# Copying the masked blocks ahead of the exponentials on ScalarE, in the fourth head of three groups

## The reference

```python
# 1: gated linear attention, 8 heads of 128
q, k = l2norm(x @ Wq), l2norm(x @ Wk)
v, alpha = x @ Wv, sigmoid(x @ Wg)
S = a_t[..., None] * S + k_t[..., None] * v_t[:, :, None, :]
o_t = einsum('bhkv,bhk->bhv', S, q_t)          # then o @ Wo
# 2: cross attention with the context
probs = softmax(x @ W.T @ ctx.T); out = probs @ ctx
# 3: two of eight small experts per sequence, chosen by a gate on the mean row
out = sum over the two of weight * (gelu(x @ down + b) @ up + b_up)
```

## Time and profile before

| | us |
|---|---|
| median of the runs | 489.06 |
| the profiled execution's own time | 488.91 |
| its span, first to last instruction | 486.8 |
| TensorE (PE) busy | 462.1 (95%) |
| VectorE (DVE) busy | 374.4 (77%) |
| ScalarE (ACT) busy | 337.6 (69%) |
| GpSimd (POOL) busy | 109.6 (23%) |
| mean granted TensorE clock | 0.988 of 2.4 GHz |

### The profile page before, as it was taken

One profiled execution on the slowest core, in us unless ns is written; L12 is line 12 of the kernel. 1 busy time (PEld: TensorE's weight loads), 2 busy tenths in 40 slices (PEclk: granted clock), 3 DMA queues, 4 the chain that ended last, 5 costly groups with the idle time before them and its releaser, 6 DMA issues. The chain is left out here.

```text
span 486.8 us, 24127 instructions
## 1 busy us (share of the span) xinstructions
PE 462.1 (95%) x10322; PEld 385.0 (79%) x10322; DVE 374.4 (77%) x1059; ACT 337.6 (69%) x800; POOL 109.6 (23%) x102
## 2 busy tenths in 40 slices
PE   1799999999999999999999999999999999999886
PEld 1588788887888788888888888887878888877674
DVE  4778896767779788896779788887579678887574
ACT  3858877766777776778757776678857776766613
POOL 1022232212222222233122221233212221232121
PEclk9989999999999999999999999999999999999979
DMA  8900000001001010013011010013010010002023
GB/s 314 349 11 5 3 5 3 5 3 44 6 3 46 3 47 4 3 49 90 3 46 47 2 48 3 3 27 109 4 46 3 4 42 7 5 25 67 0 52 123
DMA packets 15321, 20.17 MB, mean 41 GB/s; under 512 B 1264, under 2 KB 13040, under 8 KB 15216
## 3 DMA queue, kind: packets, MB, share of 16 engines
q1 hardware_dynamic: 13936, 14.43, 9.2%
q0 software_dynamic: 1280, 4.20, 3.2%
HBM read 16.53 MB, written 2.10 MB: 38 GB/s over the span
## 5 line engine op out<-in xcount | busy, mean ns | idle before, releaser
L507 ACT COPY states<-states 128x512 f32<-128x512 f32 x128 | 80.9, 632 | 54.8 <-DVE states L741 41.0
L419 POOL TENSOR_TENSOR rnorm<-norm_sq,neg_half 128x4 f32<-128x4 f32 x32 | 44.6, 1394 | 265.6 <-DVE norm_sq L804 265.6
L741 DVE TENSOR_TENSOR states<-states,spans 128x512 f32<-128x512 f32 x96 | 66.4, 692 | 8.9 <-ACT states L507 1.0
L1254 PEld LDWEIGHTS lo_bank<-states 128*32 128x32 f32 x5120 | 51.4, 110 | 23.1 <-issue 19.4
L1254 PE MATMUL lo_bank<-states 128*32 128x16 f32 (+1 forms) x5120 | 58.4, 188 | 0.0
L1243 PE MATMUL ring<-wv_sb,xnT 128*128 128x256 f32 x384 | 55.9, 295 | 1.2 <-DVE wv_sb L1010 1.0
L1230 PE MATMUL ring<-xnT,wk_sb 128*128 128x512 f32 x192 | 53.7, 416 | 2.3 <-DVE xnT L873 1.5
L1230 PE MATMUL ring<-xnT,wq_sb 128*128 128x512 f32 x192 | 53.4, 413 | 0.0
L1230 PE MATMUL ring<-xnT,wg_sb 128*128 128x512 f32 x192 | 51.3, 402 | 0.4 <-DVE wg_sb L1010 0.4
L1243 PEld LDWEIGHTS ring<-wv_sb,xnT 128*128 128x128 f32 x384 | 49.2, 193 | 1.9 <-DVE wv_sb L1010 1.1
L792 DVE COPY_PREDICATED blocks<-owned,lo_bank 128x64 f32<-128x64 uint32 (+1 forms) x160 | 41.0, 256 | 12.1 <-PE lo_bank L1254 7.6
(11 more groups left out here) (201 smaller groups left out, 834.0 us busy)
## 6 DMA issues: line engine op xcount, KB each, us to landing
x_buf<-x_dram SPq DMA_DIRECT2D x4, 512.0 KB, 4.0
ctxT_sb<-ctxT_dram SPq DMA_DIRECT2D x8, 256.0 KB, 4.1
ctx_sb<-ctx_dram SPq DMA_DIRECT2D x4, 512.0 KB, 4.3
out_dram<-x_mid SPq DMA_DIRECT2D x6, 256.0 KB, 2.5
states<-wk_dram SPq DMA_DIRECT2D x1, 1024.0 KB, 5.7
states<-wg_dram SPq DMA_DIRECT2D x1, 1024.0 KB, 7.9
states<-wq_dram SPq DMA_DIRECT2D x1, 1024.0 KB, 9.9
v_sb<-wv_dram SPq DMA_DIRECT2D x1, 1024.0 KB, 12.0
```

The lines of the kernel that those rows point to most:

```text
L419: nc.gpsimd.tensor_tensor(rnorm[:, m % 4, GB:2 * GB], norm_sq[:, GB:2 * GB], neg_half[:, GB:2 * GB], ALU.pow).then_inc(rk_set, 1)
L507: nc.scalar.copy(halves(l, 2 ** (l - 1), False), halves(l - 1, 2 ** (l - 1), False)).then_inc(carry_set, 1)
L741: nc.vector.tensor_tensor(halves(l, w, True), halves(l - 1, w, True), by, ALU.mult).then_inc(decayed, 1)
L1254: last = mm(lo_bank[BLOCK * r:BLOCK * r + BLOCK, to:to + columns], view(states, left + start, [[1, BLOCK]]), view(states, right + start, q ...
```

## The change

In the heads with h = 3 from the second group on (n = 11, 19, 27), ScalarE issues `expand_blocks(n - 1)` directly behind `carry(n, 5)`, ahead of the exponentials and of alpha. In all other heads it stays behind alpha. The instructions, their waits and the semaphores that they signal are the same; no other engine's program changes.

```diff
                 carry(n, 5)
+                blocks_first = n % H == 3 and n > H
+                if blocks_first:
+                    expand_blocks(n - 1)
                 tail_part(n, "early")
                 if n + 1 < U:
                     alpha_out(n + 1)
-                if n >= 1:
+                if n >= 1 and not blocks_first:
                     expand_blocks(n - 1)
                 tail_part(n, "mid")
```

## The result

The changed kernel takes 486.65 us (median of 22 runs, 484.24 to 492.26). The kernel before, run beside it, takes 489.42 us (median of 22, 486.97 to 493.51). The ratio is 0.9936 with a 95% interval of 0.9918 to 0.9953. Put on the 489.06 us of the first three runs that is 485.9 us (485.0 to 486.8), where 487.2 was forecast with a range of 486.5 to 488.4. The direction was right, the gain was put too small: 1.85 us, against 2.3 to 4.0 by the interval. The ratio is formed from the runs that are not over 1.5% above the fastest, and it is not the ratio of the two medians: those are 2.8 us apart, 0.9943.

What follows compares the result with a forecast made beforehand. TensorE was taken to bound the kernel, waiting at L1324 for ScalarE's square in heads 11, 19 and 27; removing 0.75 + 0.68 + 0.42 = 1.85 us from 489.06 gave 487.2 us, range 486.5 to 488.4.

Steps and rivals of the forecast that it cites:

- What bounds the kernel: TensorE, busy 95% of the span; its wait at L1324 for ScalarE's square, three times, 1.8 us in all.
- The copies in their new place: On ScalarE ahead of the exponentials, 1.21 us of copies hide in the wait for VectorE's maxima; cost 0, at most 0.3.
- The rule on the drain behind a table load: The skill's 1.38 us drain after ScalarE's table load would make the exponentials late; as a rival 488.3 us, chance 0.03.
- The place that they leave: Behind alpha on ScalarE, the square ends 1.21 us earlier, so L1324's whole wait goes: 1.85 us, bounds 1.15 to 1.85.
- What is late next: VectorE's scaled output and the split of `xT` for TensorE's next products: both stay in time, margins 0.13 and 0.31 us.
- the first rival: VectorE comes no earlier and stops L1392 for 0.35 us in heads 11 and 19; gain 1.15, 487.9 us, chance 0.07.
- The margin of 0.13: Slack left for VectorE's scaled output before TensorE's `cross` 1 needs it: 0.40 + 0.48 - 0.75 us.
- the sum's last one: Whole kernel: median 489.06 less the three waits' 1.85 gives 487.2 us, 0.38% faster; forecast's chance 0.80.
- The fifth rival: Slow clock from 468 to 477 us falls on other work: 1.6 us less (485.6) or more (488.8), chance 0.04.

Runs made afterwards that it cites:

- g_overfill: Changed kernel plus four filler copies directly behind the masked copies, ahead of the exponentials, in heads 11, 19 and 27; ratio 0.9959 to the kernel before, median 487.98 us.
- b_hold: Changed kernel plus four filler copies behind alpha, in the place the masked copies left, heads 11, 19, 27; ratio 0.9998 to the kernel before, median 489.47 us.
- c_square_first: Kernel before with the masked copies of heads 11, 19 and 27 moved later, behind q's copy and square; ratio 0.9997 to the kernel before, median 491.97 us.
- e_max_only: Kernel before, masked copies unmoved, with VectorE's row maxima ahead of the two decays in heads 11, 19, 27; ratio 0.9910 to the kernel before, median 486.12 us.
- a_same: The kernel before, unedited, run against itself to measure noise; ratio 0.9979, medians 489.60 and 489.67 us.
- h_max_only: Second run of row maxima first on VectorE, masked copies where they were in the kernel before; ratio 0.9926 to the kernel before, median 486.26 us.

## Why the prediction was wrong, point by point

- **What bounds the kernel**: right. TensorE's wait at L1324 was the only one that the change touched, and it vanished in all three heads.
- **The copies in their new place cost nothing**: right. The idle time left before the exponentials is 1.18, 1.26 and 0.41 us, for 1.16, 1.18 and 0.33 forecast. g_overfill shows that the cover is real and where it ends.
- **The rule on the drain behind a table load**: the trace decides against it. In the changed kernel's head 11 the load ends at 163.57 and the exponentials wait for the maxima; in g_overfill nothing but the load is ahead of them, and they start 0.02 us behind its end. A drain of 1.38 us as in the Trainium skill ("ScalarE: Activation LUTs", "What ACT_TABLE_LOAD costs") would have shown there.
- **The place that they leave**: the mechanism was right (b_hold, c_square_first). The term was 0.75 + 0.68 + 0.42 = 1.85 and measured 0.83 + 0.73 + 0.45 = 2.01, and 2.16 and 1.80 in two more traces. Its upper bound, 1.85 itself, was too low.
- **What is late next**: right, VectorE came earlier by itself, and the first rival did not happen. The margin of 0.13 was too careful: VectorE lost a second idle time too, 0.31 us behind line 507, and the margin stayed near the 0.40 of before.
- **The step that failed is the sum's last one, with the range built on it.** It set the end time as "489.06 - 1.85 = 487.2": everything outside the three waits was put at no change, on the ground that "The three runs lie within 0.15 us", with only 0.7 us beyond the forecast below "for smaller differences in how TensorE's groups meet". The runs showed 2.8 us in all (2.1 to 3.5) and 2.0 by the three waits, so the term that was put at nothing measured some 0.8 us; its cause stays open. The range allowed a gain of 2.6. Nor was the base as firm as it looked: the kernel before runs between 486.97 and 493.51, in the traces `o` 0 starts between 41.3 and 44.3 us, the stretch from `o` 31 to the end takes 38.2 to 40.5, and the kernel before against itself came out at 0.9979, where the prediction counted on telling 0.2% from no change. Three runs that happened to agree were taken for the spread of the program.
- **The fifth rival**, the clock at the end, was given 0.04 and a price of up to 1.6 us. Its lower value, 485.6, lay outside the stated range, and the measured 485.9 is near it; but that is no proof of it. The profile after has a shorter low stretch at the end (-0.87 us) and a longer start (+1.00), and how much of the 0.8 us is the clock's, the runs do not show.

## What to carry to other kernels

An in-order engine that waits for a late input in the middle of its program is the place for work whose own inputs are long ready. The gain is not the time moved, but the wait of the bottleneck behind it, and it is there only if all conditions of that wait move; the cover is the idle time in front of the late input, and it should be measured in the head where it is shortest. If the late input itself can be brought forward (e_max_only: one reduction earlier on VectorE), that is worth more, 2.8 us by the steps, and makes the other move needless.

For small gains the distance between two marks close to the change repeats to 0.2 us in the traces here, while the time of a whole run strays by several, and a long stretch of a trace can hold a pause of TensorE (up to 5.4 us between `o` 14 and `o` 15); both should be read.

## What the hardware showed that I had not expected

- The clock at the start is a matter of the run. Where the granted clock fell for 3.4 us within the first 32 us, `o` 0 started at 42.5 to 43.7; where it fell for 6.8, at 44.0 and 44.3; where it did not fall at all, at 41.3 to 41.4. At the end, low stretches of 3.4, 6.8 and 10.2 us go with 38.2 to 38.5, 39.1 to 39.4 and 40.5 us from `o` 31 to the last instruction.
- TensorE pauses now and then without a wait, in the middle of a row of equal products: 1.9 and 2.5 us at one place between `o` 14 and `o` 15 (a_same, h_max_only), 0.2 to 0.7 at one place between `o` 19 and `o` 20 in five of the 13 traces. The DMA packets of the trace show something beside the two long ones. A packet of the instruction queue (q8, 16 KB) that starts at 221.9 to 224.9 us in the other eleven traces started at 227.0 and 227.6 in these two, just as, and 0.4 us after, a transfer of 512 KB on another queue ended; and TensorE went on 1.2 and 1.3 us after the packet's end. So its instructions were probably late; no run tested this. A late packet does not always stop TensorE: in c_square_first one came 4 us late near 397 us without a pause.
- The clock can fall in the middle of the kernel: after the pause of 2.48 us it was low for 6.8 us, after the one of 1.93 us it stayed at its upper level.
